# Moving softplus' floor and the copy of the transposed product from ScalarE to VectorE in a Mamba and mixture-of-experts kernel

## The reference

```python
x = einsum('ed,bld->bel', in_proj_w, hidden_states)          # 512 channels e from 256
u = silu(conv_4_taps(x) + conv_b)
x_dbl = einsum('ke,bel->bkl', x_proj_w, u)                   # dt_lo (16), B (16), C (16)
delta = softplus(einsum('er,brl->bel', dt_proj_w, dt_lo) + dt_proj_b)
A = -exp(A_log)                                              # 16 decays n of each channel
state = state * exp(d_t * A) + (d_t * u_t) * B_t             # step in time, for each channel and n
y_t = einsum('ben,bn->be', state, C_t)
y = (y + D * u) * silu(z)
x = x + tanh(g) * y ;  then  x + tanh(g2) * moe(layernorm(x))
```

## Time and profile before

| | |
|---|---|
| median of three runs | 1519.1 us (1516.85 to 1519.81) |
| the profiled execution | 1513.53 us, span of its instructions 1511.8 us |
| lead | 0 to 52.24 us |
| first steps of the four batches | at 52.24, 169.27, 287.48 and 402.07 us (first `bdiag`) |
| end of the last scan | 513.6 us |
| mixture of experts | 513.6 to 1511.8 us, PE busy for 948.9 us of it |

### The profile page before, as it was taken

One profiled execution on the slowest core, in us unless ns is written; L12 is line 12 of the kernel. 1 busy time (PEld: TensorE's weight loads), 2 busy tenths in 40 slices (PEclk: granted clock), 3 DMA queues, 4 the chain that ended last, 5 costly groups with the idle time before them and its releaser, 6 DMA issues.

```text
span 1511.8 us, 32069 instructions
## 1 busy us (share of the span) xinstructions
PE 1363.4 (90%) x8344; PEld 1205.7 (80%) x8345; DVE 787.8 (52%) x1381; ACT 750.1 (50%) x1305; POOL 985.9 (65%) x685
## 2 busy tenths in 40 slices
PE   5797888888888589989999999999999999999996
PEld 2576766777778488978888989898988988898985
DVE  4789887889988923653233333333333333333331
ACT  5698897888889244223233233333333333323321
POOL 2688897898988656777455566655466655556632
PEclk8799999998999799999999999999999999999998
DMA  4030112112141054543545554445554535545332
GB/s 130 4 96 30 57 64 91 36 65 87 49 155 39 29 143 92 114 80 67 130 79 144 132 136 115 118 105 130 144 131 130 132 61 141 142 130 137 66 71 35
DMA packets 62932, 144.97 MB, mean 96 GB/s; under 512 B 16913, under 2 KB 17553, under 8 KB 60545
## 3 DMA queue, kind: packets, MB, share of 16 engines
q0 software_dynamic: 31024, 62.10, 21.6%
q1 hardware_dynamic: 31552, 77.57, 15.5%
q10 hardware_dynamic: 288, 4.46, 0.8%
HBM read 101.53 MB, written 44.80 MB: 97 GB/s over the span
## 4 chain that ended last, share of the span: by engine, by line
PE 61%; DVE 3%; issue 2%; ACT 2%; another core or an unknown queue 2%; DVEq 0%; ACTq 0%; POOLq 0%; POOL 0%
PE bank L1572 18%; PE bank L1552 17%; PE bank L1553 16%; PE bank L1540 4%; PE bank L1561 3%; PE bank L1461 1%; PE bank L1448 1%; ACT dA L738 0%; PE bank L1463 0%; DVE hs L1060 0%; DVE upto L1157 0%; ACT gt L730 0%; PE bank L1496 0%; ACT w L759 0%
## 5 line engine op out<-in xcount | busy, mean ns | idle before, releaser
L1552 PE MATMUL bank<-w,xh 128*128 (+1 forms) x1088 | 370.5, 341 | 16.6 <-issue 8.6
L856 POOL TENSOR_TENSOR hc<-hs,crow 128x512 f32<-128x512 f32 x256 | 322.3, 1289 | 71.4 <-DVE hs L1060 37.7
L1553 PE MATMUL bank<-w,xh 128*128 (+1 forms) x1088 | 352.8, 325 | 0.0
L920 POOL DMA_INDIRECT out_x<-ys,aid x104 | 172.1, 1655 | 275.3 <-issue 260.5
L1060 DVE TENSOR_TENSOR_SCAN hs<-dA,bank 128x512 f32<-128x512 f32 x256 | 293.2, 1202 | 57.4 <-PE bank L1463 28.4
L1572 PE MATMUL bank<-w,ah 128*128 (+1 forms) x816 | 268.4, 410 | 7.6 <-DVE al L1275 7.2
L1275 DVE TENSOR_TENSOR al<-bank,ah 128x384 fp32r<-128x384 f32 x136 | 75.8, 557 | 332.9 <-ACT ah L784 294.1
L1552 PEld LDWEIGHTS bank<-w,xh 128*128 128x128 f32 x1088 | 205.5, 189 | 47.9 <-issue 37.9
L774 ACT CAST xh<-bank 128x512 fp32r<-128x512 f32 x136 | 79.8, 587 | 276.6 <-PE bank L1540 238.5
L1553 PEld LDWEIGHTS bank<-w,xh 128*128 128x128 f32 x1088 | 207.6, 191 | 1.9
L1461 PE MATMUL bank<-ident,gt 128*128 128x128 f32 x768 | 144.0, 300 | 51.9 <-DVE hs L1060 34.6
(11 more groups left out here) (172 smaller groups left out, 2183.6 us busy)
## 6 DMA issues: line engine op xcount, KB each, us to landing
wraw<-in_wall SPq DMA_DIRECT2D x16, 2176.0 KB
crow<-c_rows SPq DMA_DIRECT2D x64, 256.0 KB, 3.3
xt<-token_rows SPq DMA_DIRECT2D x32, 257.0 KB
wraw<-in_wall ACTq DMA_DIRECT2D x2, 2176.0 KB
token_rows<-rowb SPq DMA_DIRECT2D x4, 1028.0 KB
xrow<-in_x SPq DMA_DIRECT2D x4, 1024.0 KB, 7.7
out_x<-xrow SPq DMA_DIRECT2D x4, 1024.0 KB
ctxt<-in_ctxT SPq DMA_DIRECT2D x4, 512.0 KB, 4.1
```

Source lines behind the costliest of these rows:

```text
L856: nc.gpsimd.tensor_tensor(hc[:, j, :], hs[:, j, :], crow[:, n % 4, :], ALU.mult).then_inc(hc_done, 1)
L920: pool.indirect_dma_start(out_rows, bass.IndirectOffsetOnAxis(ap=which, axis=0), ys[:, s, :], None, bounds_check=TOKENS - 1, oob_is_err=Fa ...
L1552: nc.tensor.matmul(gate_bank[:, 0:I], xx, columns(w, off + ww + k * 2 * I, I), start=first, stop=last)
L1553: mm = nc.tensor.matmul(up_bank[:, 0:I], xx, columns(w, off + ww + k * 2 * I + I, I), start=first, stop=last)
```

## The change

ACT's `decay` no longer makes the floor: it does Abs and Exp alone. DVE makes the floor from the same bank with one instruction (new function `floor`), after ACT's Abs has read it, and it is now the floor that frees the bank. POOL's first addition waits for that instead of for `floor_done`. The copy of the transposed product into `duT` is no longer on ACT but on DVE, as a plain copy. And the tables of PE, ACT, DVE and POOL are written anew; SP's are as they were.

```diff
@@ scalar
-                nc.scalar.activation(delta[q % 2][:, j, :], of_first("dt", j, q)[:], ACT.Relu, bias=dtbias[:, j:j + 1]).then_inc(floor_done, 1)
-                nc.scalar.activation(sw[:, j, :], of_first("dt", j, q)[:], ACT.Abs, bias=dtbias[:, j:j + 1]).then_inc(gone[bank], 1)
-                act.wait_ge(gone[bank], m + 1)
+                nc.scalar.activation(sw[:, j, :], of_first("dt", j, q)[:], ACT.Abs, bias=dtbias[:, j:j + 1]).then_inc(abs_done, 1)
+                act.wait_ge(abs_done, J * q + j + 1)
                 nc.scalar.activation(sw[:, j, :], sw[:, j, :], ACT.Exp, scale=-1.0).then_inc(se_done, 1)
...
-            def dut(q, j):
-                bank, m = use("dut", j, q)
-                apart(act, full[bank], m + 1, "act")
-                nc.scalar.copy(duT[q % 2][:, :, j * P:(j + 1) * P],
-                               misc[bank][:].rearrange("p (c t) -> p c t", t=P)).then_inc(gone[bank], 1)
@@ gpsimd, delta_
-                pool.wait_ge(floor_done, i + 1)
+                bank, m = use("dt", j, q)
+                pool.wait_ge(gone[bank], m + 1)
@@ vector
+            def floor(q, j):
+                bank, m = use("dt", j, q)
+                dve.wait_ge(abs_done, J * q + j + 1)
+                if j == 0:
+                    at_least(dve, dA_done, DS * J * (q - 1))
+                nc.vector.tensor_scalar(delta[q % 2][:, j, :], of_first("dt", j, q)[:], dtbias[:, j:j + 1], 0.0, ALU.add,
+                                        ALU.max).then_inc(gone[bank], 1)
+
+            def dut(q, j):
+                bank, m = use("dut", j, q)
+                dve.wait_ge(full[bank], m + 1)
+                if j == 0:
+                    at_least(dve, g_done, DS * (q - 1))
+                nc.vector.tensor_copy(duT[q % 2][:, :, j * P:(j + 1) * P],
+                                      misc[bank][:].rearrange("p (c t) -> p c t", t=P)).then_inc(gone[bank], 1)
@@ tables, two of the lines as an example
-DVE_FIRST = {1: [("inproj", "pre", 1)], 2: [("inproj", "pre", 2)], 4: [("inproj", "pre", 3)], 6: [("excess", "pre", 0), ("excess", "pre", 1)],
+DVE_FIRST = {1: [("inproj", "pre", 1)], 3: [("inproj", "pre", 2)], 4: [("inproj", "pre", 3)],
+             6: [("floor", "pre", 0), ("excess", "pre", 0), ("nmr", "both", 0), ("floor", "pre", 1)], 7: [("floor", "pre", 2), ("excess", "pre", 1)],
```

More of the change, by code:

```diff
@@ new lines @@
+ACT_SECOND = {1: [("xproj", "pre", 0)],
+              2: [("decay", "pre", 0), ("decay", "pre", 1), ("decay", "pre", 2), ("softplus", "pre", 0), ("softplus", "pre", 1)],
+              3: [("decay", "pre", 3)], 6: [("rstd", "both", 0)], 7: [("inproj", "next", 0), ("bt", "pre", 0), ("norm", "epi", 0)],
+              8: [("softplus", "pre", 2), ("inproj", "next", 1)], 9: [("xlt", "epi", 0), ("xlt", "epi", 1)],
+              10: [("softplus", "pre", 3), ("inproj", "next", 2)], 11: [("xlt", "epi", 2), ("inproj", "next", 3)], 12: [("xlt", "epi", 3)],
+              13: [("silu", "next", 0), ("siluz", "own", 0), ("table", "own", 0)], 14: [("szt", "own", 0)],
+              15: [("szt", "own", 1), ("szt", "own", 2), ("gate", "epi", 0), ("szt", "own", 3)]}
@@ new lines @@
+ACT_THIRD = {2: [("xproj", "pre", 0), ("decay", "pre", 0)], 3: [("decay", "pre", 1)], 5: [("rstd", "both", 0)],
+             6: [("softplus", "pre", 0), ("decay", "pre", 2), ("decay", "pre", 3), ("softplus", "pre", 1)], 8: [("norm", "epi", 0)],
+             9: [("bt", "pre", 0)],
+             10: [("xlt", "epi", 0), ("softplus", "pre", 2), ("siluz", "own", 0), ("table", "own", 0), ("xlt", "epi", 1), ("xlt", "epi", 2), ("xlt", "epi", 3)],
+             11: [("softplus", "pre", 3)], 13: [("szt", "own", 0)],
+             15: [("gate", "epi", 0), ("szt", "own", 1), ("szt", "own", 2), ("szt", "own", 3)]}
@@ new lines @@
+DVE_THIRD = {0: [("y", "epi", 0)], 1: [("x2", "epi", 0), ("x2", "epi", 1)],
+             2: [("floor", "pre", 0), ("floor", "pre", 1), ("excess", "pre", 0), ("x2", "epi", 2), ("x2", "epi", 3)],
+             4: [("stats2", "epi", 0), ("nmr", "both", 0)], 5: [("excess", "pre", 1), ("excess", "pre", 2)],
+             6: [("floor", "pre", 2), ("gate", "late", 1), ("delta", "pre", 0), ("floor", "pre", 3)], 9: [("excess", "pre", 3), ("delta", "pre", 1)],
+             10: [("delta", "pre", 2), ("gate", "late", 2)], 11: [("delta", "pre", 3), ("dut", "pre", 0)],
+             12: [("gate", "epi", 0), ("stats", "pre", 0), ("dut", "pre", 1)], 13: [("dut", "pre", 2)], 14: [("dut", "pre", 3)]}
@@ new lines @@
+DVE_LAST = {0: [("y", "epi", 0)], 1: [("x2", "epi", 0)],
+            3: [("x2", "epi", 1), ("x2", "epi", 2), ("x2", "epi", 3), ("stats2", "epi", 0), ("nmr", "both", 0)], 7: [("gate", "late", 1)],
+            11: [("gate", "late", 2), ("gate", "epi", 0)], 13: [("rank", "last", 0)],
+            15: [("gate", "end", 1), ("match", "last", 0), ("gate", "end", 2), ("match", "last", 1)]}
+POOL_LEAD = {0: [("delta", "pre", 0), ("delta", "pre", 1), ("du", "pre", 0), ("du", "pre", 1), ("delta", "pre", 2), ("delta", "pre", 3), ("du", "pre", 2), ("du", "pre", 3)]}
@@ L383, in mamba_moe @@
         tap_done = sem("tap_done")
-        floor_done = sem("floor_done")
+        abs_done = sem("abs_done")
         raised = sem("raised")
```

115 lines of the change are left out of this document (48 added, 67 removed).

## The result

| | before | after |
|---|---|---|
| median, 8 runs each on one chip | 1516.38 us (1514.59 to 1519.81) | 1505.53 us (1498.46 to 1510.25) |
| ratio, 95% interval | | 0.9921 (0.9899 to 0.9942) |
| profiled execution, and its span | 1513.5, 1511.8 us | 1509.0, 1507.2 us |

The change is faster, by 10.9 us between these medians. Three further comparisons gave 0.9950 (0.9926 to 0.9973), 0.9946 (0.9925 to 0.9967) and 0.9949 (0.9920 to 0.9979): 5.4, 6.4 and 8.3 us by their medians. The mean of the four is 7.7 us; I take 5 to 11 as what the change is worth. The eight runs of after fall into two sets, four at 1508.2 to 1510.3 us and four at 1498.5 to 1502.8, and the profiled execution is of the first.

A forecast was written before the change was run, and what follows sets the result against it. First part bound by ACT, DVE and POOL taking turns, through each queue over a step or two; second part by PE. Batches -4.7 plus lead +0.9 gave -3.8 us: median 1515.3 us, range 1506 to 1526.

The forecast's parts named there:

- queues' prices: Batches 0 to 2: floors and copies at 0.62 us each add 5.0 us a batch to DVE; ACT loses 4.4.
- cap rule: First part's batches: no engine filled beyond 0.91 of a batch, so 458.2 us in all, 4.7 less than before.
- batch 0 gains nothing: Batch 0: no gain, since a new heap of 12.8 us stands on DVE behind step 8.
- batches 1 and 2 shorter together by 3 to 6 us: Batches 1 and 2: sign of a right forecast, both shorter, together by 3 to 6 us.
- Batch 3 the same within 1: Batch 3, which has neither moved operation: sign of a right forecast, its time unchanged within 1 us.
- it lies 5.6 us below the median, so I forecast the median as 1519.1 - 3.8: Whole kernel: profiled execution forecast at 1509.7 us, carried to a median of 1515.3 by before's 5.6 us offset.
- pair rule: First part: a step takes half of the fullest engine's queue over it and the next step; 10.4 us less.
- The lead: Before the first scan: cover for DVE's statistics and dskm is gone, first scan near 55.0 us, 0.9 later.
- DVE as the bound: Batches 0 to 2: DVE filled to only 0.88, +7.3 us with the lead, 1526.4 us; chance 0.26.
- Banks held longer: dt banks wait for the floor in DVE's queue, delaying PE: +4.2 us, net +0.4, 1519.5 us; chance 0.22.
- Spreading in full: First part: pair rule without cap, -10.4 us, and a lead 0.5 shorter: 1508.2 us; chance 0.17.
- The second part: Second part, 998.2 us before: nothing added; the forecast fails if it changes by more than 1 us.

The follow-up runs named there:

- e0: The kernel before, run again unchanged: 1494.8 us against before's 1493.47, ratio 1.0002.
- e1: The changed kernel, run again beside before on one chip: 1488.11 us against 1493.47, ratio 0.9950.
- e14: The kernel before with the copies alone on DVE at the old places and the change's last-batch tables: 1515.76 us against 1516.06, ratio 0.9993.
- e15: The changed kernel with the last batch's late gate piece back at step 9 instead of 11: 1506.31 us against before's 1516.06, ratio 0.9916.
- e3: The kernel before with both floor and copy on DVE, at the old places: 1508.6 us against 1492.98, ratio 1.0101.
- e10: The kernel before with the floor alone on DVE, at the old places: 1507.23 us against 1493.24, ratio 1.0090.
- e2: The kernel before with only the last batch's four tables (PE, ACT, DVE, POOL) from the change: 1490.01 us against 1493.47, ratio 0.9970.
- e4: The changed kernel with floor and copy both back on ACT, at the new places: 1495.85 us against before's 1493.47, ratio 1.0004.
- e5: The changed kernel with only the floor on DVE, the copy back on ACT: 1499.28 us against before's 1492.98, ratio 1.0041.
- e9: The kernel before with the copy alone on DVE, at the old places: 1492.89 us against 1493.24, ratio 0.9994.
- e6: The changed kernel with only the copy on DVE, the floor back on ACT: 1486.94 us against before's 1492.98, ratio 0.9956.
- e13: The changed kernel with the last batch's tables of before: 1511.13 us against before's 1516.06, ratio 0.9962.

## Why the prediction fell short

**The direction and the queues' prices were right.** Copies were priced at 0.62 us and cost 0.61, floors 0.62 and cost 0.65. ACT is busy 4.2, 3.8 and 4.2 us less in batches 0 to 2 (forecast 4.4). The Trainium skill, "VectorE: DVE Perf Modes", section "The TRN2 errata", has 120 cycles plus one for each element at 0.96 GHz for VectorE out of a bank, from which I estimate 0.66 us for this size. The floor's distance, 0.65, agrees with that estimate, the copy's 0.61 lies below. One price isn't the one used: silu stands at 8.0 among the prices and at 7.5 in the queues (step 12 before has 4.6 + 0.5 + 0.5 + 7.5 = 13.1), before and after alike.

**The sum of the first part had the level right and the gain too large.** The cap rule gave 118.4, 115.4, 114.7 and 109.7 us, in all 458.2. Four profiles of the changed kernel have 115.5, 116.2, 114.8 and 111.6 on average, 458.0; two of before have 460.7, where the rule had 462.9, so it is 2.7 us less and not 4.7. By batches it was wrong: "batch 0 gains nothing" (it gained 2.3 and 0.0 us on the same and on another chip), and "batches 1 and 2 shorter together by 3 to 6 us" (0.4 in the first pair of profiles, 2.7 in e0 and e1). "Batch 3 the same within 1" failed in the first pair, by 3.5 us, and held for the average of the profiles.

**The step that failed is "it lies 5.6 us below the median, so I forecast the median as 1519.1 - 3.8".** It takes for granted that a profiled execution stands as far from the median in both kernels, and it rests on a median of three runs. Of the 9.8 us between 1515.3 and 1505.53, 2.7 are that base: eight runs put before's median at 1516.38. Only 0.8 are the sum's: between the two profiled executions the gain was 4.6 us (1513.53 to 1508.97), with 3.8 forecast. The other 6.3 are the offset: before's profiled execution lies 2.9 us under its median of eight, the changed kernel's 3.4 us above. It is so in the later groups too: e0 5.3 us under, the changed kernel 0.0, 4.3 and 4.0 us above (1488.11 for 1488.11; 1491.14 for 1486.81; 1512.41 for 1508.45). So a gain of 2.7 us in the batches of the profiles and of 7.7 in the medians belong to one change. The other pair of profiles from one chip, e0 and e1, differs by 1.4 us, so that the forecast of the profiled execution came within 0.8 us is in part luck.

**What the offset goes with is the mean granted clock of TensorE,** which is on record with each execution. Within a kernel an execution is shorter the higher that clock is: for the 30 runs of before in the first group the correlation is -0.94 and the slope 1.07 us for each 0.001, for the four sets of the changed kernel -0.92 to -0.97 and 1.3 to 1.5 us. e0's profiled execution had 0.963, with 0.9585 as the median of its twelve; those of the changed kernel had 0.958, 0.961, 0.958 and 0.958, with medians of 0.9605, 0.961, 0.963 and 0.9595. Over all 19 sets of runs the offset follows this distance with a correlation of -0.90, 1.2 us for each 0.001; e14's -6.2 us came with +0.005 and e15's +7.0 with -0.004. Profiles of before were thus taken at a high clock (the first at 0.960, with none on record for the other runs beside it) and those of the changed kernel mostly at a low one.

The gain itself goes with it in part. In the three groups that hold both, the changed kernel has a mean clock of 0.9617, 0.9622 and 0.9595, before 0.9592, 0.9593 and 0.9566. By the slopes this is an estimate of about 3 us of mean gains of 7.2, 8.1 and 7.6, and the forecast has no term for it. In e3 and e10, the slow ones, the clock is low as well, 0.9536 and 0.9547, for 0.9598 and 0.9593 in before beside them. In e2 it is 0.9625, by the slope an estimate of all its 3.5 us. All this is correlation: whether a kernel in which PE waits less gets the higher clock, or the clock shortens the waits, no run separates.

**The pair rule sees queues and not waits.** It counts what stands in each queue and asks nothing about what an instruction waits for. With the same prices, applied to the tables of the experiments, it gives -1.0 us for e10 (measured +14.0), -1.7 for e3 (+15.6), -9.9 for e4 (+2.4) and -10.0 for e5 (+6.3), while it is near for e9 (-0.7 for -0.4) and e6 (-10.3 for -6.0 and -9.5). It fails where an instruction stands ahead of another engine's data, or ahead of its own. That it fitted the four batches of before was no test of this. In e4 it puts the gain down to the places alone, and they are worth nothing without the mix.

**The lead** was forecast 0.9 us later, at 55.0, and the first scan began at 54.16 as before. The chain was right, and one term of it was the most of the error: dskm was priced at 1.87 us from the earlier trace rows, where POOL was at work, and took 0.87 where POOL was idle.

**The rivals.** DVE as the bound: batch 1 is filled to 0.88 (103.67 of 117.54) as that rival said, batches 0 and 2 to 0.91, and the kernel isn't slower. The slower side exists all the same, in e3 and e10, through waits of ACT and PE and not through DVE's fill. Banks held longer: scans would wait for PE longer than 28.4 us and waited 17.0, so in the changed kernel it was not that. At the old places it is real: in e10 PE stands 6.80 us for a bank that a floor holds, 2.88 in e0. Spreading in full, 1508.2: nearest to the median, but its sum, -10.4 in the first part, is in no profile of the changed kernel.

**The second part** changed by 1.5 us, outside the 1 us I gave, with nothing of the change in it. Between profiles of the changed kernel on like chips it varies by more (977.9 and 975.8; 999.7 and 1002.2), and in e13, which has the same second part, it took 1007.0.

## What to carry to other kernels

Price a moved operation by the wait that it makes in its in-order queue and by what is queued behind that wait, on the engine it leaves as well as on the one it joins: here the move of 0.5 us copies was worth 6 us or more in one set of tables and nothing in another, and that of 0.65 us floors cost 14 us or nothing. Ask also which bank or tile the moved operation frees, and who stands for it. A rule that adds up queues should be tried on a variant that is known to be bad before it is believed. A profiled execution is one draw; put its granted clock beside that of the other runs before a gain of a few us is carried from it to the median.
